# Decoder layer with a mixture of experts: the inverse of the token routing is computed ahead of step 10, with its products on GpSimd

## The reference, cut to what matters

```python
shared = jnp.einsum('ti,hi->th', silu(x @ sh_gate_w.T) * (x @ sh_up_w.T), sh_down_w)
probs = softmax(x @ router_weight.T)
top_v, top_i = jax.lax.top_k(probs, 2)
combine = (one_hot(top_i, 8) * (top_v / top_v.sum())[..., None]).sum(axis=1)
for e in range(8):
    gate, up = split(x @ gate_up_proj[e].T)
    out = out + (silu(gate) * up @ down_proj[e].T) * combine[:, e:e + 1]
out = out + sigmoid(x @ shared_gate_w.T) * shared
x = layernorm(x + out)
```

## Time and profile before

| what | us |
|---|---|
| median of 3 runs | 1759.94 |
| lowest and highest of them | 1757.28, 1761.05 |
| the profiled execution's own time | 1747.85 |
| its span | 1746.0 |
| TensorE busy in it | 1689.4 (97%) |
| VectorE busy | 1227.4 (70%) |
| ScalarE busy | 931.1 (53%) |
| GpSimd busy | 662.0 (38%) |

### The profile page before, as it was taken

One profiled execution on the slowest core, in us unless ns is written; L12 is line 12 of the kernel. 1 busy time (PEld: TensorE's weight loads), 2 busy tenths in 40 slices (PEclk: granted clock), 3 DMA queues, 4 the chain that ended last, 5 costly groups with the idle time before them and its releaser, 6 DMA issues.

```text
span 1746.0 us, 28868 instructions
## 1 busy us (share of the span) xinstructions
PE 1689.4 (97%) x10034; PEld 1518.4 (87%) x10034; DVE 1227.4 (70%) x3381; ACT 931.1 (53%) x1707; POOL 662.0 (38%) x417
## 2 busy tenths in 40 slices
PE   6999899999999999999999999999999999998996
PEld 5788788999898998989898999898998989988985
DVE  4655577777777777777878777877777787747557
ACT  4433255565656556565656565656556565644542
POOL 1111153333434335253433333434334251253525
PEclk9999999999999999999999999999999999998998
DMA  5034463323232324241423323232324230441423
GB/s 194 32 117 144 144 148 95 55 75 67 62 67 62 67 74 71 70 87 52 89 42 87 48 85 67 62 67 62 67 71 70 73 67 12 106 116 31 132 79 100
DMA packets 102856, 140.29 MB, mean 80 GB/s; under 512 B 37022, under 2 KB 81728, under 8 KB 102592
## 3 DMA queue, kind: packets, MB, share of 16 engines
q1 hardware_dynamic: 60784, 115.47, 26.0%
q10 hardware_dynamic: 38912, 14.80, 3.9%
q0 software_dynamic: 3024, 8.26, 1.7%
HBM read 113.62 MB, written 24.89 MB: 79 GB/s over the span
## 4 chain that ended last, share of the span: by engine, by line
PE 87%; DVE 6%; DMA 4%; ACT 1%; issue 1%; POOL 1%; SPq 0%; POOLq 0%; ACTq 0%; DVEq 0%
PE b_turn L767 16%; PE b_out L786 9%; PE b_out L787 9%; PE b_out L788 9%; PE b_score L753 9%; PE b_score L755 8%; PE b_score L754 8%; PE b_out L796 5%; PE a_bank L324 3%; PE c_gate L1447 2%; PE c_down L1474 1%; DMA rden_store<-b_rden 1%; PE a_bank L344 1%; DMA a_x<-in_x 1%; PE a_bank L364 1%
## 5 line engine op out<-in xcount | busy, mean ns | idle before, releaser
L831 ACT CAST b_pT_hi<-b_turn 125x512 fp32r<-125x512 f32 (+1 forms) x768 | 406.5, 530 | 545.1 <-PE b_turn L767 543.6
L933 DVE TENSOR_TENSOR b_pT_lo<-b_turn,b_pT_hi 125x512 fp32r<-125x512 f32 (+1 forms) x768 | 477.8, 623 | 266.4 <-ACT b_pT_hi L831 261.5
L919 DVE CUSTOM_DVE_ANT_0 b_p<-b_score,b_mask_add 128x500 f32<-128x500 f32 x672 | 452.0, 673 | 62.9 <-PE b_turn L767 23.6
L767 PEld LDWEIGHTS b_turn<-ident,b_p 128*125 128x125 f32 x2688 | 409.8, 186 | 55.8 <-ACT b_p L837 0.5
L767 PE MATMUL b_turn<-ident,b_p 128*125 128x128 f32 x2688 | 418.6, 272 | 0.2 <-ACT b_p L837 0.2
L837 ACT ACTIVATE b_p<-b_p,b_shift 128x1500 f32<-128x1500 f32 x224 | 347.5, 1551 | 5.3 <-DMA rden_store<-b_rden 3.0
L786 PE MATMUL b_out<-b_pT_hi,b_c_hi 125*128 125x512 f32 (+1 forms) x768 | 346.8, 452 | 3.0 <-DVE b_pT_lo L933 3.0
L1071 POOL TENSOR_TENSOR b_oT_lo<-b_oT,b_oT_hi 128x896 fp32r<-128x896 f32 x32 | 67.6, 2113 | 625.7 <-ACT b_oT_hi L861 589.2
L787 PE MATMUL b_out<-b_pT_lo,b_c_hi 125*128 125x512 f32 (+1 forms) x768 | 281.1, 366 | 0.0
L788 PE MATMUL b_out<-b_pT_hi,b_c_lo 125*128 125x512 f32 (+1 forms) x768 | 280.8, 366 | 0.0
L753 PE MATMUL b_score<-b_cT_hi,b_q_hi 128*128 128x500 f32 x672 | 263.4, 392 | 0.0
(11 more groups left out here) (248 smaller groups left out, 2403.5 us busy)
## 6 DMA issues: line engine op xcount, KB each, us to landing
cT_in<-in_ctxT SPq DMA_DIRECT2D x32, 750.0 KB, 10.3
b_c_in<-in_ctx SPq DMA_DIRECT2D x32, 750.0 KB
q_store<-a_fold_in_or_q_stage SPq DMA_DIRECT2D x16, 896.0 KB, 4.2
q_in<-q_store SPq DMA_DIRECT2D x32, 448.0 KB, 6.2
b_rden_all<-rden_store ACTq DMA_DIRECT2D x32, 256.0 KB, 5.5
b_rden_all<-rden_store ACTq DMA_DIRECT2D x32, 192.0 KB, 3.6
b_mask_in<-in_mask SPq DMA_DIRECT2D x32, 187.5 KB, 9.7
slot_store<-c_y2T SPq DMA_DIRECT2D x35, 128.0 KB, 2.0
```

Of the source, the lines that this page charges most:

```text
L767: mm = pe.transpose(turn_bank[n % 3][0:CK, u * 128:(u + 1) * 128], p[slot % 2][:, u, c * CK:(c + 1) * CK], ident[:])
L831: act.copy(pT_hi[:, n % 3, 0:w], turn_bank[n % 3][0:CK, 0:w]).then_inc(hi_done, 1)
L919: dve.tensor_tensor_reduce(out=p[slot % 2][:, u, keys], in0=score_bank[j][:, 0:FW], in1=mask_add[:, b, keys], scale=1.0, scalar=-3.0e38, o ...
L933: dve.tensor_tensor(pT_lo[:, n % 3, 0:w], turn_bank[n % 3][0:CK, 0:w], pT_hi[:, n % 3, 0:w].bitcast(F32), ALU.subtract).then_inc(lo_done, 1)
```

## The change

The two products of `match_tiles` move from VectorE to GpSimd, in a new function `tokens_of_tiles` behind the split of the last weight that GpSimd splits whole, ahead of the first fetch. `match_places` comes a step sooner on VectorE (steps 7 and 8). `invert()` moves on TensorE from behind the loop to the head of step 10, with a wait for both products; `sources()` moves on VectorE to the head of step 10 as well. The counter's marks are renumbered.

```diff
-        inverted = sem("inverted")
+        inverted, at_tile_done = sem("inverted"), sem("at_tile_done")
...
-        PLACED, MATCHED, TABLE_DONE, SOURCED = 33, 41, 44, 45
+        PLACED, PASSED, MATCHED, SOURCED, TABLE_DONE = 33, 37, 39, 40, 43
...
+        INVERT_AT = GA - 2
...
             def invert():
 
+                pe.wait_ge(at_tile_done, 2)
                 pe.wait_ge(route_chain, MATCHED)
...
                 if turning == 3:
                     turn_y2(3, 0)
+                if g == INVERT_AT:
+                    invert()
                 hidden(g, 0)
...
-            invert()
             for g in range(GA - LAG, GA):
                 down(g)
...
-                for j in range(2):
-                    link(dve.tensor_tensor(at_tile[:, j], passed[:, j], token.unsqueeze(2).to_broadcast([128, NT, RP]), ALU.mult))
+                assert done == PASSED
...
+                if g == INVERT_AT:
+                    sources()
                 gated(g)
...
                 if g == 7:
                     split_slots()
                     match_tiles()
-                if g in (8, 9):
-                    match_places(g - 8)
+                if g in (7, 8):
+                    match_places(g - 7)
                 if g == 10:
                     tile_table()
-            sources()
             for p in BY_VECTOR:
                 expert_rest(p)
...
+            def tokens_of_tiles():
+
+                pool.wait_ge(route_chain, PASSED)
+                for j in range(2):
+                    pool.tensor_tensor(at_tile[:, j], passed[:, j], token.unsqueeze(2).to_broadcast([128, NT, RP]),
+                                       ALU.mult).then_inc(at_tile_done, 1)
...
             for p in range(SC, SC + WHOLE):
                 split(p)
+            tokens_of_tiles()
             for s in range(X_DEEP):
                 fetch_x(s)
```

## The result

| | before | after |
|---|---|---|
| median of the runs compared, us | 1758.63 (14 runs) | 1763.02 (14 runs) |
| profiled execution: own time / span | 1747.85 / 1746.0 | 1759.89 / 1758.1 |
| TensorE's mean granted clock | 0.992 | 0.987 |

The ratio is 1.0026, with a 95% interval of 1.0014 to 1.0037: the change costs 4.4 us, and the interval runs from 2.5 to 6.5. The two spans differ by 12.1 us, and the 4.4 of the medians can't be all of that. The profile of before is an unusually short execution: its own time lies 7 us under the lowest of its 14 runs (1754.97). Nor do the two profiles reach the changed place at the same time: the tile match starts at 1582.23 in the one and at 1574.61 in the other, 7.6 us apart, before anything that the change touches.

What follows compares the result with a forecast made beforehand. TensorE's chain of waits was taken as the bound. Later first expert, contention included (+1.4), inverse at low clock (+2.6), steps behind it (+1.7) and saving (-0.8) gave +4.9 us on 1759.94: 1764.8, range 1757.5 to 1769.5.

Steps and rivals of the forecast that it cites:

- The one-hots: VectorE's chain behind the tile match: the second one-hot was to end 3.0 us sooner than before.
- Contention, +0.9: GpSimd's second product was to hold up VectorE's second one-hot by 0.9 us, so the inverse starts at 1590.1.
- the rival in which the two engines queue in full: Products go first, both one-hots end late, the inverse starts at 1591.7: +6.5 us, 1766.4; chance 0.13.
- The standstill: TensorE ahead of the inverse was to stand still for 4.3 us (bounds 3.4 and 6.0).
- The inverse at low clock: After the standstill, the inverse's matmuls were to take 5.8 us at half clock instead of 3.2: +2.6 us.
- The rival in which the 36-column matmuls keep their pace: The clock falls, but the inverse is bound by issue and no slower: +2.3 us, 1762.2; chance 0.18.
- rows 5: Windows with granted clock in the profile of before; the prediction read no fall there where TensorE was dense.
- The steps behind it: Steps 10, 11 and the `down`, 8.6 us at full clock, were to begin at low clock: +1.7 us.
- The tail: VectorE's work behind the last `down` was to delay the first expert by 3.1 us, to 1605.0 at full clock.
- Behind the reference point, -0.8: Behind the first expert tile, the earlier 1.7 us low-clock loss might vanish or recur; saving taken as 0.8 us.
- The rival in which the clock holds: The clock stays at 2.4 GHz through the wait ahead of the inverse: -1.2 us, 1758.7; chance 0.13.

Runs made afterwards that it cites:

- ahead of step 11: The changed kernel with the inverse and the source list at the head of step 11 instead of 10: 1760.92 us, ratio 1.0001 to the kernel before.
- the filled wait: The changed kernel with 15 needless 512-column matmuls ahead of the inverse's wait: 1763.8 us, ratio 1.0007 to the kernel before.
- both profiles of before: The unchanged kernel's first profile (1747.85 us) and a second one taken in the follow-ups, nothing changed: 1764.88 us.

## Why the prediction was right

Forecast 1764.8 us against 1759.94, that is +4.9; measured +4.4, with the interval 2.5 to 6.5. By its steps:

- **The one-hots.** Predicted end of the second, 3.0 us sooner: it came 3.0 sooner.
- **Contention, +0.9.** The order came as forecast: the first product waited behind the first one-hot (2871 against 1028 ns), and the second was still running when the second one-hot was due. Too large was the length of the products. The step took 1.26 us for each, from rows of 512 columns, so that the second would end 2.5 us behind the first one-hot; it ended 1.9 behind it (1579.76 - 1577.87), since the first needed 0.89 there and the second 1.03. That left an overlap of 0.2 us with the second one-hot instead of 0.9, and it lost 0.07. The term should have been 0.1, and the rival in which the two engines queue in full did not come. The Trainium skill (GPSIMD Engine Reference, section 1) names contention with VectorE's instructions of two SBUF inputs, and the 2871 ns agree. Which engine yields, the traces show: the one that begins second. Here that was GpSimd's first product, in the earlier trace rows VectorE's operation.
- **The standstill.** 4.3 predicted, 3.49 measured, for that reason: the lower bound of 3.4 was the right one.
- **The inverse at low clock.** +2.6 predicted from the experts' factor of 1.8, +2.93 measured, a factor of 1.9. The rival in which the 36-column matmuls keep their pace is refuted: 6.13 / 28 = 0.219 us for each against 3.20 / 28 = 0.114. One remark beside this step was misread: rows 5 were said to show no fall where TensorE was dense. They show one: TensorE was busy for 3.40 of 3.40 us in the window that ends where the clock fell, and it went on working.
- **The steps behind it.** From the end of the inverse to the last `down` took 10.3 us against 8.6 worked out: +1.7, as predicted. The windows show 3 us at 0.50, then 0.99.
- **The tail.** 3.1 us predicted between the last `down` and the first expert; 3.2 measured, and released by VectorE's `x_rest` (now L1807) as forecast. The fetches left the path. (The reading of before was slightly off: the last `down` ended at 1598.72 + 0.41 = 1599.13, so the hole was 4.5 us and not 4.7. The sum does not use it.)
- **Behind the reference point, -0.8.** Wrong: the clock fell a second time in the tail, and the low stretch came again (0.58 from 1601.3 to 1605.4). The saving was 0. The step named this as one of two ways and took the middle.

With its terms as measured the sum is 0.5 + 2.9 + 1.7 + 0 = +5.1, with 0.1 for contention and 0.1 for the tail +5.3, beside +5.4 at the third tile. So two errors, 0.8 too much for contention and 0.8 too much saving, cancelled by luck, while the large terms stood. The mechanism, standstill and low clock, is the one forecast.

The rival in which the clock holds is refuted for this kernel by both its profiles. That it is possible elsewhere the runs show: ahead of step 11, without a wait, it held. On the clock, the Trainium skill (TensorE: Matmul & The Clock Gate, Part 1) lets the gate follow how busy the array has been. For the standstill that agrees (granted 0.89 in the idle window, 0.50 behind it). In the filled wait the profile's busy share does not show it: TensorE was busy for 2.48 of 2.50 us in the window in which the clock began to fall, and for all 1.70 us of the next, at 0.50. That share adds up the durations of the matmuls and does not say how busy the array was within them, so this fall neither bears the rule out nor refutes it.

What stays open: how the 4.4 us divide between standstill and clock in unprofiled runs, why the clock fell in the filled wait and held ahead of step 11, and why the gain of 2.2 us ahead of step 11 does not show in its time.

## What to carry to other kernels

Work that feeds a later stage is moved up only as far as its inputs let it run without a wait: one step too far cost 4.4 us here, one step less cost nothing. On TensorE a wait costs more than its length, since the matmuls behind it can run at half clock; of 3.15 us head start all but 0.2 was lost that way. Ask before such a move what is late next (here VectorE's queue ahead of the first expert), and clear that too: the only certain gain, 5.8 us, came with the inverse one step later and that queue shortened.

## What the runs showed of the hardware

- The clock can fall inside a dense run of short matmuls. It did so in the filled wait, 2.2 us into the 36-column matmuls, and in both profiles of before about 1 us behind them, with TensorE still working; in four experiments it held through the same 28 matmuls. So such a run does not always bring the fall, and what decides is not shown.
- GpSimd's multiply that began beside a VectorE instruction with two inputs from SBUF took 2871 ns instead of 1028, and ended at 1578.76, 0.89 us behind VectorE's at 1577.87: it did hardly any of its 1.03 us of work meanwhile. Outside such an overlap, at 504 columns, it was faster than the 1280 ns of the 512-column rows I had taken for it.
- In nine of ten profiles TensorE stalls for some 5 to 6.5 us in all near 1620 to 1635, and again in steps of 0.3 to 2.4 us near 1708 to 1726, where the trace names no releaser. In the tenth, the first of before, they are absent, and its span is 12 to 22 us shorter. Their cause was not looked for.
